# Moving the decay sums, two conv projections and a pair of copies in the Mamba stage of a macaron block

## What is computed

```python
x = x + 0.5 * ffn(layernorm(x), router_w, w1, w2)
x = x + mamba(layernorm(x), ...)
x = x + 0.5 * ffn(layernorm(x), router_w, w1, w2)

# mamba, 8 heads of 64, state 64, conv of 4 taps, 640 conv channels
zxbcdt = x @ W_in
dt = softplus(dt + dt_bias)
xBC = silu(conv4(xBC) + conv_b)
s = s * exp(dt * A) + dt * x * B        # per token, head
y = s @ C + D * x
y = y * silu(z)
y = y * rsqrt(mean(y * y) + EPS) * norm_weight
out = y @ W_out
```

## Time and profile before

| | |
|---|---|
| median of 3 runs | 1248.7 us (1247.84 to 1250.36) |
| the profiled execution's own time | 1249.26 us |
| its span, first to last instruction | 1247.5 us |
| PE busy | 1012.6 us (81%) |
| PE weight loads busy | 860.8 us (69%) |
| DVE busy | 738.8 us (59%) |
| ACT busy | 606.3 us (49%) |
| POOL busy | 596.8 us (48%) |
| mean granted TensorE clock | 0.926 of full speed |

### The profile page before, as it was taken

The page is one execution under the profiler, slowest core; times in us unless marked ns, Lnnn a source line. Parts: engine busy times, 40 slices in busy tenths (PEclk is TensorE's granted clock), DMA queues, the critical chain, the costliest instruction groups (busy, mean ns, idle before and its releaser), DMA issues. The chain is left out here.

```text
span 1247.5 us, 21987 instructions
## 1 busy us (share of the span) xinstructions
PE 1012.6 (81%) x6624; PEld 860.8 (69%) x6656; DVE 738.8 (59%) x1614; ACT 606.3 (49%) x1568; POOL 596.8 (48%) x612
## 2 busy tenths in 40 slices
PE   3746999999974788988888888888737999999960
PEld 3745999999963566766666666666526999999950
DVE  6975444444436868678788777765365444444437
ACT  1323555555532455465655656565424555555530
POOL 6922555555522236354545454547503555555520
PEclk9998999999995689799999999999858999999985
DMA  7872222322313101011111110000062223322339
GB/s 229 278 301 75 73 77 77 96 77 77 79 42 107 50 27 46 22 54 37 59 43 43 43 39 18 18 18 26 30 278 63 91 96 93 97 91 95 92 115 324
DMA packets 73259, 112.22 MB, mean 90 GB/s; under 512 B 10680, under 2 KB 60352, under 8 KB 71872
## 3 DMA queue, kind: packets, MB, share of 16 engines
q1 hardware_dynamic: 48704, 60.48, 14.6%
q0 software_dynamic: 13824, 37.77, 9.5%
q10 hardware_dynamic: 10624, 12.58, 3.0%
HBM read 66.76 MB, written 44.04 MB: 89 GB/s over the span
## 5 line engine op out<-in xcount | busy, mean ns | idle before, releaser
L427 POOL DMA_INDIRECT ys_d<-xs,row_of x144 | 142.5, 989 | 194.6 <-DVE xs L811 188.9
L491 ACT ACTIVATE hs<-pH 128x512 f32<-128x512 f32 x144 | 86.1, 598 | 229.5 <-PE pH L613 229.5
L422 POOL DMA_INDIRECT xs<-xn_d,token_of x144 | 140.0, 972 | 114.2 <-DVE token_of L785 70.9
L800 DVE TENSOR_TENSOR xl<-pT,xh 128x256 fp32r<-128x256 f32 x144 | 61.1, 425 | 221.3 <-ACT xh L504 221.0
L805 DVE TENSOR_TENSOR h2l<-hs,h2h 128x512 fp32r<-128x512 f32 x144 | 99.8, 693 | 77.1 <-ACT h2h L499 76.9
L1615 DVE SCALAR_TENSOR_TENSOR acc<-bank,cwh,acc 128x511 f32<-128x511 f32 (+2 forms) x120 | 89.6, 747 | 43.6 <-ACT acc L1224 40.8
L633 PE MATMUL pY<-w2h,h2h 128*128 x576 | 103.3, 301 | 0.5 <-DVE h2l L805 0.4
L1128 POOL TENSOR_TENSOR yv<-yv,sz 128x512 f32<-128x512 f32 x32 | 40.7, 1271 | 116.7 <-DVE yv L1657 113.5
L613 PE MATMUL pH<-w1h,xh 128*128 x288 | 92.6, 403 | 1.8 <-DVE xl L800 1.1
L613 PE MATMUL pH<-w1l,xh 128*128 x288 | 92.1, 402 | 0.0
L633 PE MATMUL pY<-w2h,h2l 128*128 x576 | 91.1, 280 | 0.0
(11 more groups left out here) (255 smaller groups left out, 2581.0 us busy)
## 6 DMA issues: line engine op xcount, KB each, us to landing
m_yg<-ys_d SPq DMA_DIRECT2D x64, 128.0 KB, 2.2
xs<-ys_d SPq DMA_DIRECT2D x12, 512.0 KB, 6.6
wst<-in_L_ffn_w_dram ACTq DMA_DIRECT2D x8, 512.0 KB, 4.5
xs<-in_L_attn_x_dram SPq DMA_DIRECT2D x8, 512.0 KB, 6.3
hs<-in_L_ffn_w_dram ACTq DMA_DIRECT2D x8, 512.0 KB, 4.8
xn_d<-xs SPq DMA_DIRECT2D x8, 512.0 KB, 3.3
lo_d<-w1l SPq DMA_DIRECT2D x1, 4096.0 KB, 11.8
lo_d<-w2l SPq DMA_DIRECT2D x1, 4096.0 KB, 21.4
```

The lines of the kernel that those rows point to most:

```text
L422: pool.indirect_dma_start(out=xg[:, t % NX, :], out_offset=None, in_=xn_d, in_offset=bass.IndirectOffsetOnAxis(ap=token_of[:, t:t + 1], ax ...
L427: pool.indirect_dma_start(out=ys_d, out_offset=bass.IndirectOffsetOnAxis(ap=row_of[:, t:t + 1], axis=0), in_=y[:, t % NX, :], in_offset=No ...
L491: act.activation(r[:, u, :], pH[u][:, :], ACT.Relu).then_inc(relu_done.sem, 1)
L800: dve.tensor_tensor(xl[:, u, :, :], src, xh[:, u, :, :].bitcast(F32), ALU.subtract).then_inc(g_split.sem, 1)
```

## The change

Four places of the same function are written in another order; no instruction is added, removed or altered.

- DVE: `sum_up` stands behind `scale_state`, ahead of the taps of the TAPPED block, the silu of the HANDED one, both additions of the input, the residual and the moments.
- PE: the early projection stands ahead of `turn_b` and `turn_xc`.
- PE: the late projection stands behind dt of kind 0 and `turn_x2`.
- ACT: the first taps of the early block stand ahead of `copy_b` and `copy_x`.

```diff
@@ ACT @@
+                for B in blocks(s, EARLY):
+                    first_taps(*B)
                 if live(s + 1):
                     copy_b(s + 1)
                     copy_x(s + 1)
-                for B in blocks(s, EARLY):
-                    first_taps(*B)
@@ PE @@
                     within(s)
                     to_state(s)
+                for B in blocks(s, EARLY):
+                    project(*B)
                 if live(s + 1):
                     turn_b(s + 1)
                     turn_xc(s + 1)
-                for B in blocks(s, EARLY):
-                    project(*B)
...
                     project_z(s + 2)
-                for B in blocks(s, LATE):
-                    project(*B)
                 if live(s + 8) and s % GC == 0:
...
                     turn_x2(s - 2, s)
+                for B in blocks(s, LATE):
+                    project(*B)
@@ DVE @@
                     scale_state(s)
+                if cum_group(s) is not None:
+                    sum_up(cum_group(s))
                 for B in blocks(s, TAPPED):
                     convolve(*B)
...
                     spread(s + 10)
-                if cum_group(s) is not None:
-                    sum_up(cum_group(s))
                 if live(s):
                     add_within(s)
```

## The result

The changed kernel takes 1253.66 us (median of 20 runs, 1250.95 to 1258.11) against 1250.26 us of the kernel before on the same chip (20 runs): ratio 1.0033, 95% interval 1.0022 to 1.0043. It is slower by about 3.4 us.

A forecast was written before the change was run, and what follows sets the result against it. No engine is full, so hand-overs between engines bound the block. Seven groups at 0.45 us (3.2) plus 2.4 for the filling add 5.6 us to the profiled 1249.26; less 0.56 to the median, 1254.3 us, range 1247 to 1260.

The forecast's parts named there:

- PE's wait at `turn_b`: Kind-0 slot: the early projection fills PE's 1.08 us wait for the sums; nothing of it is left at the y transpose.
- The CAST held by POOL: Kind-0 slot: POOL's L1123 holds DVE's CAST in the early sums, 0.75 us, so the sums take 1.81 us.
- Rival 1: The sums are not held by POOL; a group gains 0.25 us: 1249.4 us, no change, chance 0.18.
- ACT's order: Kind-0 slot: copies wait for ACT's first tap, so the y transpose waits for copy_x and comes 0.8 us later.
- The late projection: Kind-0 slot: on PE it starts 2.96 us behind the y transpose, at 700.4 in place of 700.19.
- the kind-0 slot: First slot of four (s % 4 = 0): next state product 0.55 us earlier, ACT's late block 0.2 later, carried on.
- The group: Four slots of the running block: 0.45 us slower each, over seven groups 3.2 us.
- The kind-1 slot: Slot with s % 4 = 1: 0.8 us longer, from ACT's later part and the late projection behind yT.
- The filling: Slots before chunk 0: DVE waits for ACT's totals, so the first state product comes 2.4 us later, bounds 1.0 to 3.2.
- Rivals 3 and 4: 3: PE's longer pause costs clock, 1259.5 us, chance 0.10. 4: chunk 4's low-clock stretch falls away, 1249.1 us, chance 0.07.
- Rival 2: PE is the bound; its wait at turn_b goes, 7.6 us gained, 2.4 lost: 1243.5 us, chance 0.15.

The follow-up runs named there:

- split: Changed kernel, but the CAST and L1599 go back to their old place and only the first three of the five sums stand early: 1249.28 us.
- copies_first: Changed kernel with only ACT's order put back, copies of B and x ahead of the first tap: 1256.64 us.
- pe_only: Kernel before with both PE projection moves alone, ACT and DVE as before: 1249.04 us.
- late_back: Kernel before with only the early projection moved ahead on PE and the first tap moved ahead of the copies on ACT: 1240.26 us.
- fill_old: Changed kernel, but in the slots ahead of chunk 0 the decay sums stay behind the taps as before: 1249.31 us.
- tap_first_k0: Changed kernel with the DVE sums at their old place, and in kind-1 slots ACT's copies ahead of the first tap as before: 1252.31 us.
- early_only: Kernel before with only the early projection moved ahead of turn_b on PE: 1260.94 us.

## Why the prediction was right, and where it was not

The number (1254.3 us), the sign and the range held. Some of its steps did not, and that the number came within 0.6 us is luck.

*PE's wait at `turn_b`*, as forecast: gone, with nothing left of it at the y transpose. *The CAST held by POOL*, as forecast: 0.94 us where I wrote 0.80 or more, `add_within` 0.73 later for 0.75, and split shows that this was on the path of the kind-0 slot. The taps end 0.15 us behind to_state by the numbers of the prediction itself (692.6 and 692.45), which it called "just before"; PE waits 0.23 us for them. The rule that I quoted from the Trainium skill (SBUF — State Buffer, Who interferes with whom) is borne out here: seven of eight CASTs, those of the running block, take 0.93 to 1.23 us; the one in the filling, where POOL does nothing, takes 0.20. That it ends 0.08 us after L1123 fits a lock held for the whole instruction. Rival 1 has fallen.

*ACT's order*, as forecast: the y transpose waits for L1239, 10.26 us after the state product for the 10.3 forecast. In the working I took this wait as the cost of the tap's move. The runs show that beside the early projection the tap ahead costs a kind-0 slot nothing: with the copies first the y transpose is 0.6 us earlier, but the late projection, which follows the taps, is 0.2 us later in copies_first and 0.8 in pe_only.

*The late projection* came at 12.91 us of the slot for 13.27 forecast. The failed term is the stretch from the y transpose to it: I added 2.96 us, and it took 2.65. The y transpose and z took what was forecast (1.87 for 1.86). The small dt products took 0.58 for 0.80: the 0.80 was read between two weight loads, of which the first runs 0.22 us ahead of its matmul and the second does not. The 0.1 for a hand-over was not needed, since PE runs through without a pause. After it come 2.04 us (2.05 forecast). So the kind-0 slot is 1.0 us shorter, for 0.55. The error of 0.36 goes on: ACT gets the late block 0.17 us earlier (14.59 us into the slot for 14.76 before), where I carried 0.2 later, and in chunk 17 the copy yT ends 29.32 us after the group's first state product, for 29.70 forecast and 29.50 before.

*The group* follows from that: 0.45 us forecast, and 0.01 measured in chunks 16 to 19. Four of the seven groups (first chunk 0, 12, 16, 24) lie within 0.2 us of those before; that of chunk 4 is 3.3 us shorter and those of chunks 8 and 20 are 0.9 and 2.2 longer, with other stretches at half clock than before. The step that failed is thus "seven groups have the early and late blocks: 7 x 0.45 = 3.2 us slower", and 0.37 of the 0.45 is the term carried over from the kind-0 slot. *The kind-1 slot*, 0.8 longer, was right (0.82), with its two causes, ACT's later part and the late projection behind yT; late_back, which lacks the second, has it at 15.2.

*The filling*, 2.4 forecast, 2.88 measured; fill_old confirms that it makes the loss, since without it the change is level with the kernel before. Measured terms give 2.9 + 0.1 = 3.0 us, and the medians differ by 3.4; I forecast 5.6. That 1254.3 was still so near to 1253.66 has a second reason: the median that it started from, 1248.7 us of 3 runs, lies 1.6 under the 1250.26 of the 20 runs beside the change. A group term that was 3.2 too large, a filling 0.5 too small and a start 1.6 too low left an error of 0.6. The prediction's bounds also add up to 1251.1 to 1257.5, not to the 1250.1 to 1258 written; the range doesn't hang on it.

*Rivals 3 and 4*, which I had given 0.10 and 0.07, both happened in part in the profiled execution. Chunk 4's slot went from 21.2 us to 15.8, but chunks 5, 9 and 21 take 17.73, 17.43 and 18.91 against 16.67, and from the last state product to the end it is 365.2 us against 358.8, with a clock of 0.58 in the first 20.8 us. The span is 8.9 us longer than before, and 6.4 of that lie behind the last state product. No instruction stands in another order there, yet this stretch is 361.6 to 365.3 us in the traces of all twelve other kernels. With one trace of the kernel before, it can't be told whether its 358.8 is usual, nor what of the 6.4 is in the median.

*Rival 2* (PE is the bound, 1243.5 us) was wrong for the change, but its gain is there in the early projection and the tap together: late_back gains 9.4 us. My argument against it was that the sums put `norm` at 693.90; in late_back, which leaves the sums where they were, copy_x is done at 9.3 us of the slot and the y transpose starts at 9.4, before's 9.5.

What stays open is why a pause of PE of 1.8 to 2.3 us is followed by half clock in one slot and not in a like one, and why half clock also comes without such a pause. The runs show all of this, and no experiment separated the cause.

## What to carry to other kernels

Try the parts of a reordering one at a time and in pairs: here two of four moves belong together and are worth 9 us, each alone shows as a loss, and the other two hide the gain. An instruction on DVE that is small by itself can be held for a whole POOL instruction when it is moved next to one, so look at what POOL does at the new place and not at the duration at the old one. And check a move that is meant for the steady state in the filling too, where its inputs come late: there the same lines cost 2.9 us, and a condition on the slot takes that back.

## What the runs showed of the hardware

- The CAST of 32x128 from fp32 to bf16 took 0.18 to 0.21 us alone and 0.93 us when it began 0.41 us after POOL's 1.27 us tensor_tensor (1.24 where it began 0.10 after it): it ends 0.07 to 0.08 us after POOL's instruction.
- The granted clock falls to half in stretches of a few us up to most of a slot, in versions whose PE work is the same 6656 matmuls. One slot's time differed by this from 15.16 to 16.72 us for the same order of instructions, and from 14.1 to 19.8 for another. Three of my expectations (tap_first_k0, pe_only, early_only) missed by 9 to 20 us; in two of them, tap_first_k0 and early_only, it is these stretches that the windows show. In early_only five slots (chunks 1, 4, 5, 20 and 21) are 4 to 7 us longer than an undisturbed slot of their kind. tap_first_k0 ran from 1239.76 to 1254.86 us in 12 runs. So I would judge a change of less than about 5 us in this kernel by the undisturbed slots as well as by the median.
